# Cross attention scores in 32-row tiles, one query head of each key group at a time, in a two-layer decoder on one core

## The reference

```python
hidden = jnp.concatenate([context, latents], axis=1)
q = (latents @ Wq.T).reshape(b, q_len, H, HD)
k = (hidden @ Wk.T).reshape(b, s_len, KV, HD)
v = (hidden @ Wv.T).reshape(b, s_len, KV, HD)
...
scores = jnp.einsum('bkgqd,bksd->bkgqs', q, k) * scale
attn = jax.nn.softmax(scores.astype(jnp.float32), axis=-1).astype(q.dtype)
out = jnp.einsum('bkgqs,bksd->bkgqd', attn, v)
...
return out @ Wo.T
```

## Time and profile before

| What | Value |
|---|---|
| median of 3 runs | 852.35 us (851.16 to 854.41) |
| the profiled execution, its own time | 849.07 us |
| its span, first to last instruction | 847.3 us |
| instructions | 22622 |
| mean granted TensorE clock | 0.998 of full speed |
| data moved by DMA | 36.77 MB, mean 43 GB/s |
| cross attention trips, from the timeline | about 495 to 830 us |

### The profile page before, as it was taken

One profiled execution on the slowest core, in us unless ns is written; L12 is line 12 of the kernel. 1 busy time (PEld: TensorE's weight loads), 2 busy tenths in 40 slices (PEclk: granted clock), 3 DMA queues, 4 the chain that ended last, 5 costly groups with the idle time before them and its releaser, 6 DMA issues.

```text
span 847.3 us, 22622 instructions
## 1 busy us (share of the span) xinstructions
PE 812.5 (96%) x9288; PEld 673.8 (80%) x9288; DVE 574.4 (68%) x1510; ACT 432.6 (51%) x1109; POOL 262.2 (31%) x310
## 2 busy tenths in 40 slices
PE   6999999999999999999998999999999999999996
PEld 6888887675557787777776789988989899989993
DVE  5675666586876666677776547983767566756776
ACT  4454444568763343465555446634644475347532
POOL 0221522579976532112222567710000100010001
PEclk9999999999999999999999999999999999999999
DMA  8410002222221200010000122320000010000001
GB/s 306 142 53 16 16 22 83 66 70 56 72 63 38 63 22 9 20 29 18 19 19 19 32 62 89 100 65 26 1 2 2 1 50 2 2 1 27 2 2 50
DMA packets 20998, 36.77 MB, mean 43 GB/s; under 512 B 3200, under 2 KB 7424, under 8 KB 20640
## 3 DMA queue, kind: packets, MB, share of 16 engines
q1 hardware_dynamic: 20800, 35.20, 13.6%
q10 hardware_dynamic: 96, 0.13, 0.1%
HBM read 30.86 MB, written 2.10 MB: 39 GB/s over the span
## 4 chain that ended last, share of the span: by engine, by line
PE 78%; DVE 10%; ACT 4%; issue 2%; POOL 2%; DMA 2%; SPq 1%; ACTq 0%; POOLq 0%; DVEq 0%
PE bank L833 18%; PE bank L835 16%; PE bank L834 16%; PE bank L984 6%; PE bank L1259 5%; PE bank L1004 2%; PE bank L1121 2%; DVE tank L2565 2%; PE bank L989 2%; DVE tank L2345 1%; PE bank L954 1%; PE bank L1108 1%; PE bank L1243 1%; DMA x_all<-x_dram 1%; PE bank L1278 1%
## 5 line engine op out<-in xcount | busy, mean ns | idle before, releaser
L833 PE MATMUL bank<-wr,hTl 128*128 128x512 f32 (+3 forms) x392 | 153.5, 391 | 1.3 <-issue 0.8
L835 PE MATMUL bank<-wr,hTh 128*128 128x512 f32 (+3 forms) x392 | 147.0, 375 | 0.0
L834 PE MATMUL bank<-wr,hTh 128*128 128x512 f32 (+3 forms) x392 | 146.6, 374 | 0.0
L1562 ACT ACTIVATE pT<-bank 128x512 f32<-128x512 f32 x128 | 70.0, 605 | 94.9 <-PE bank L954 94.9
L2345 DVE TENSOR_REDUCE tank<-bank 128x4 f32<-128x512 f32 x128 | 82.0, 682 | 42.4 <-PE bank L954 42.4
L833 PEld LDWEIGHTS bank<-wr,hTl 128*128 128x128 f32 (+1 forms) x392 | 73.7, 188 | 17.7 <-issue 5.3
L835 PEld LDWEIGHTS bank<-wr,hTh 128*128 128x128 f32 (+1 forms) x392 | 73.7, 188 | 12.6
L834 PEld LDWEIGHTS bank<-wr,hTh 128*128 128x128 f32 (+1 forms) x392 | 73.8, 188 | 11.3 <-issue 1.0
L833 PE MATMUL bank<-hTh,wr 128*128 128x256 f32 (+1 forms) x272 | 82.0, 302 | 0.0
L834 PE MATMUL bank<-hTl,wr 128*128 128x256 f32 (+1 forms) x272 | 81.3, 299 | 0.0
L835 PE MATMUL bank<-hTh,wr 128*128 128x256 f32 (+1 forms) x272 | 81.2, 298 | 0.0
(11 more groups left out here) (257 smaller groups left out, 1923.8 us busy)
## 6 DMA issues: line engine op xcount, KB each, us to landing
raw<-w_qkv_dram SPq DMA_DIRECT2D x12, 256.0 KB, 2.8
raw<-w_xq_dram SPq DMA_DIRECT2D x16, 192.0 KB, 2.3
raw<-w_xo_dram SPq DMA_DIRECT2D x12, 256.0 KB, 2.8
cin<-xT_dram SPq DMA_DIRECT2D x8, 256.0 KB, 3.6
x_all<-x_dram SPq DMA_DIRECT2D x8, 256.0 KB, 7.0
cin<-ctx_dram SPq DMA_DIRECT2D x8, 256.0 KB, 3.4
cin<-ctxT_dram SPq DMA_DIRECT2D x8, 256.0 KB, 2.9
out_dram<-x_all SPq DMA_DIRECT2D x8, 256.0 KB, 2.0
```

Source lines behind the costliest of these rows:

```text
L833: mm(dst, lhs[1], rhs[0], start=start, stop=False)
L834: mm(dst, lhs[0], rhs[1], start=False, stop=False)
L835: return mm(dst, lhs[0], rhs[0], start=False, stop=stop)
L1562: av(pT[e][:, 2 * rows + n, :], t_bank[n][:, :], ACT.Exp).then_inc(exp_ready, 1)
```

## The change

A turn now takes one query head of each of the four key groups instead of the four heads of one group. The 96 features of a head are cut into three parts of 32, and the weights are put in such an order that a projected tile of 128 rows holds one part of all four groups. The scores of group n then use rows 32n to 32n+31 of the array and have a PSUM bank of their own, `scores_bank(n)`, for both slots: 72 matmuls of 32x256 for each turn. Keys are split once for each trip, with the factor 96^-0.5 already in them, so the maxima are negated in the reduction. The rescaled copy of the maxima, the splits of keys in each turn and the pieces of the fourth head go.

The values of a turn go to `bank[s][2]` (in the last turn `bank[s][0]`), which brings new waits. The kept values of slot 0, n = 1, move behind the queries of turn 1 in trips 1 to 3. The first half of the transposes is copied by VectorE behind its split of the queries, the second by ScalarE; in turn 2 ScalarE's `xT_copied` comes behind these copies, as in the code. In trip 0 the division of slot 1 is shared with ScalarE in every turn, before in turn 0 only. Ahead of `first_pair`, TensorE multiplies a tile of zeros (bf16, 128x512) 17 times.

```diff
...
-WIDE, NARROW = 64, 32
+PART = P // XKV
+PARTS_OF_HEAD = XD // PART
...
+        xk_last = sb("xk_last", [P, 2, SLOTS, XT], F32R)
...
+        xk_parts = [nc.alloc_sbuf_tensor_at(f"xk{c}", [P, 2, SLOTS, XT], F32R, offset=at_tank + 4 * c * TANK) for c in range(2)] + [xk_last]
...
+        xq_parts = [wr[:, at:at + PARTS_OF_HEAD * XT].rearrange("p (c s t) -> p c s t", c=PARTS_OF_HEAD, s=SLOTS) for at in (AT_AL, AT_BL)]
...
+        def rows_of_group(n):
+            return slice(n * PART, (n + 1) * PART)
+        def scores_bank(n):
+            return bank[n // SLOTS][n % SLOTS]
+        def values_bank(s, g):
+            return bank[s][2 if g + 1 < XG else 0]
...
+        CLOCKED = 17
...
+            def keep_clocked():
+                pe.wait_ge(idle_ready, 1)
+                for _ in range(CLOCKED):
+                    mm(t_bank[0][:, :], idle[:, :], idle[:, :].unsqueeze(1).broadcast_to([P, KT, P]), start=True, stop=True, skip_group_check=True)
...
+                        if g > 1:
+                            for s in both:
+                                pe.wait_ge(xo_ready[s], nth(trip, XG, g - 1))
...
+            def cross_scores(trip, g):
+                pe.wait_ge(xk_ready, nth(trip, PARTS_OF_HEAD, PARTS_OF_HEAD))
+                pe.wait_ge(xq_ready, nth(trip, XG, g + 1))
+                for q_lo, k_lo in ((1, 0), (0, 1), (0, 0)):
+                    q = xq_of(trip, g)[q_lo]
+                    for c in range(PARTS_OF_HEAD):
+                        for s in both:
+                            for n in range(XKV):
+                                at = rows_of_group(n)
+                                ins = mm(scores_bank(n)[:, s * XT:(s + 1) * XT], q[at, c, s, :], xk_parts[c][at, k_lo, s, :],
+                                         start=q_lo == 1 and c == 0 and s == 0, stop=q_lo + k_lo == 0 and c + 1 == PARTS_OF_HEAD,
+                                         skip_group_check=True)
+                ins.then_inc(xs_psum, 1)
+            def cross_probsT(trip, s, g):
+                pe.wait_ge(xp_ready[1], nth(trip, 2 * XG, 2 * g + 1 + s))
                 for i in range(2):
+                    pe.wait_ge(xpn_ready[s], nth(trip, 2 * XG, 2 * g + i + 1))
+                    if (trip, s, i) == (0, 1, 1):
+                        pe.wait_ge(first_normed, g + 1)
                     for j in range(4):
                         at = (4 * i + j) * P
                         ins = nc.tensor.transpose(bank[s][i][:, j * P:(j + 1) * P], xp[s][:, at:at + P], ident[:, :])
                     ins.then_inc(xpT_psum[s], 1)
             def cross_values(trip, s, g):
+                pe.wait_ge(xpT_ready[s], nth(trip, 2 * XG, 2 * g + 2))
                 if g == 0:
                     pe.wait_ge(xv_ready[s], nth(trip, 2, 2))
+                if g + 1 < XG:
+                    pe.wait_ge(xq_ready, nth(trip, XG, g + 2))
+                if g + 2 == XG and trip > 0:
+                    pe.wait_ge(xT_hi[s], turned(trip - 1, FF))
+                for c in range(PARTS_OF_HEAD):
                     for t in range(2):
+                        for n in range(XKV):
+                            at = t * NKV + n * XD + c * PART
+                            ins = mm(values_bank(s, g)[rows_of_group(n), c * P:(c + 1) * P], xv[s][:, at:at + PART],
+                                     xpT[s][:, (2 * n + t) * P:(2 * n + t + 1) * P], start=t == 0, stop=t == 1)
                 ins.then_inc(xo_psum[s], 1)
...
             def routes_and_low(trip, s):
                 pe.wait_ge(xT_hi[s], turned(trip, FF))
+                if trip + 1 < TRIPS:
+                    pe.wait_ge(xo_ready[s], nth(trip + 1, XG, XG - 1))
...
+            keep_clocked()
             first_pair()
...
                 cross_keys(trip)
-                if behind:
-                    cross_kept_values(trip, 1, 1)
-                cross_kept_values(trip, 0, 1)
+                cross_kept_values(trip, 1 if behind else 0, 1)
                 for g in range(XKV):
-                    each(cross_scores, trip, g)
+                    cross_scores(trip, g)
                     if g + 1 < XKV:
                         cross_q(trip, g + 1)
+                        if g == 0 and behind:
+                            cross_kept_values(trip, 0, 1)
                     elif behind:
                         each(routes_and_low, trip - 1)
                     if g > 0:
...
             def cross_keys(trip):
                 for n_done, i in enumerate(KEY_TILES):
+                    act.wait_ge(xk_psum, nth(trip, PARTS_OF_HEAD, n_done + 1))
+                    av(xk_parts[i][:, 0, :, :], bank[i % 2][i // 2][:, :].rearrange("p (s t) -> p s t", s=SLOTS), ACT.Copy, scale=XD ** -0.5
+                       ).then_inc(xk_hi, 1)
...
                 hi = xq_of(trip, g)[0]
                 act.wait_ge(xq_psum, n + 1)
                 act.wait_ge(xq_ready, nth(trip, XKV, g))
+                copy(hi[:, 0:2, :, :], two_parts(trip, g))
                 act.wait_ge(xq_psum, n + 2)
+                copy(hi[:, 2, :, :], third_part(trip, g)).then_inc(xq_hi, 1)
+            def cross_probs(trip, g):
+                if (trip, g) == (0, 0):
+                    act.wait_ge(xs_psum, 1)
+                for n, s in ((0, 0), (0, 1), (1, 0), (1, 1), (2, 0), (3, 0), (2, 1), (3, 1)):
+                    act.wait_ge(xmax_ready, nth(trip, XKV * XG, XKV * g + n + 1))
+                    ins = av(xp[s][:, n * XT:(n + 1) * XT], scores_bank(n)[:, s * XT:(s + 1) * XT], ACT.Exp,
+                             bias=st[s][:, NEGMAX.start + n:NEGMAX.start + n + 1], scale=1.0,
+                             accum_out=st[s][:, ROWSUM.start + n:ROWSUM.start + n + 1])
+                    if n % 2 == 1:
+                        ins.then_inc(xp_ready[s], 1)
+            def first_norm(g):
+                act.wait_ge(first_sums, g + 1)
                 for j in range(2, 4):
                     block = xp[1][:, j * XT:(j + 1) * XT]
                     ins = av(block, block, ACT.Copy, scale=st[1][:, ROWSUM.start + j:ROWSUM.start + j + 1])
                 ins.then_inc(first_normed, 1)
+            def second_probsT(trip, s, g):
+                act.wait_ge(xpT_psum[s], nth(trip, 2 * XG, 2 * g + 2))
+                copy(xpT[s][:, 512:1024], bank[s][1][:, :]).then_inc(xpT_ready[s], 1)
             def cross_heads(trip, s, g):
                 act.wait_ge(xo_psum[s], nth(trip, XKV, g + 1))
                 n = XG * XD // P
+                copy(hTh[:, 0:n, s, 0, :], tiles(values_bank(s, g)[:, 0:XG * XD], n)).then_inc(xo_hi[s], 1)
...
                 cross_keys(trip)
-                if behind:
-                    cross_kept_values(trip, 1, 1)
-                cross_kept_values(trip, 0, 1)
+                cross_kept_values(trip, 1 if behind else 0, 1)
                 if trip > 1:
                     each(ff_norm, trip - 2)
                 for g in range(XKV):
-                    each(cross_probs, trip, g)
-                    if g == 0:
-                        cross_split(trip, 0, 1)
+                    cross_probs(trip, g)
+                    if trip == 0:
+                        first_norm(g)
                     if g + 1 < XKV:
                         cross_q(trip, g + 1)
                     elif behind:
                         each(route_exp, trip - 1)
-                    if (trip, g) == (0, 0):
-                        first_norm()
+                    if g == 0 and behind:
+                        cross_kept_values(trip, 0, 1)
+                    each(second_probsT, trip, g)
                     for s in both:
-                        if copied_by_act(trip, s, g):
-                            probsT_by_act(trip, s, g)
-                    for s in both:
-                        if g + 1 < XKV and (g, s) != (0, 0):
-                            cross_split(trip, s, g + 1)
                         if g + 2 == XKV and behind and s == 0:
                             each(xT_copied, trip - 1, 2)
                         cross_heads(trip, s, g)
...
+            nc.gpsimd.memset(idle[:, :], 0.0).then_inc(idle_ready, 1)
...
+                v.tensor_tensor(lo[:, 0:2, :, :], two_parts(trip, g), f32(hi[:, 0:2, :, :]), ALU.subtract)
+                v.tensor_tensor(lo[:, 2, :, :], third_part(trip, g), f32(hi[:, 2, :, :]), ALU.subtract).then_inc(xq_ready, 1)
+            def cross_keys(trip):
+                for n_done, i in enumerate(KEY_TILES):
+                    dve.wait_ge(xk_hi, nth(trip, PARTS_OF_HEAD, n_done + 1))
+                    v.scalar_tensor_tensor(out=xk_parts[i][:, 1, :, :], in0=bank[i % 2][i // 2][:, :].rearrange("p (s t) -> p s t", s=SLOTS),
+                                           scalar=XD ** -0.5, in1=f32(xk_parts[i][:, 0, :, :]), op0=ALU.mult, op1=ALU.subtract
+                                           ).then_inc(xk_ready, 1)
+            def cross_max(trip, g):
+                dve.wait_ge(xs_psum, nth(trip, XG, g + 1))
+                for n in range(XKV):
```

(44 more changed lines are left out.)

112 lines of the change are left out of this document (19 added, 93 removed).

## The result

| | Before | After | Ratio (95%) |
|---|---|---|---|
| first comparison, medians (4 runs each) | 851.75 us | 843.43 us | 0.9904 (0.9886 to 0.9922) |
| both run again, medians (23 and 5 runs) | 852.02 us | 844.31 us | 0.9905 (0.9884 to 0.9927) |
| first profiled executions, own time | 849.07 us | 842.99 us | |
| profiled executions of the repeats, own time | 852.05 us | 845.23 us | |

The change makes the kernel 8 us faster, about 0.95%. The forecast was 4.6 us, 847.8. The result lies in the range, near its lower end.

The account below looks back on a forecast made before the run. TensorE, busy 812.5 of 847.3 us, was taken as the bound. Terms -8.3 - 1.1 + 3.2 + 1.6 = -4.6 us took the profiled 849.07 to 844.5; adding 3.3 to the median gave 847.8, range 842.5 to 853.5.

Parts of the forecast that it names:

- scores, 16 turns: Cross attention scores on four row tiles: stage 2.35 us instead of 2.91, in turn 0 2.45 instead of 2.84; 8.3 us gained.
- transposes, 9 turns: Turns 0, 1 and 3 of trips 1 to 3: ScalarE copying half removes a 0.12 us wait each; 1.1 us gained.
- turn 2, trips 1 to 3: Values of slot 0 wait for ScalarE's `xT_copied`, queued behind `second_probsT`: 3.05 us after the first transpose, not 1.98; 3.2 us lost.
- trip 0, waits: VectorE's slow scalings beside GpSimd delay turns 0 and 3, turn 2's wait goes; 1.6 us lost, bounds 1.3 gained, 4 lost.
- zeros: Before the first pair: zeros may save 1.5 us of slow matmuls, but TensorE then idles waiting for VectorE; nothing gained.
- profiled execution to median, before and after alike: Whole kernel: the median 852.35 lies 3.3 us above the profiled execution, so 844.5 becomes a forecast of 847.8.
- rival C: Scores: rounds are longer because stationary tile loads lie in the open; +9.6, in all +5.0 us, 857.4; chance 0.12.
- one slow pair and the key splits: Turn 2 of trip 0: VectorE's load falls by these, so the 1.28 us wait goes.
- Rival D: Start of the kernel: zeros do bring time, 1.5 us reaching the first scores; -6.1 us, 846.3; chance 0.05.
- A: Cross attention: no new waits of weight, turn 2 waits little and trip 0 nothing; about -9.7 us, 842.7; chance 0.15.
- B: Softmax chain comes late in turns 0 and 3 of every trip, 0.6 us each; about 852; chance 0.20.

Follow-up runs that it names:

- the last run: Kernel after, with VectorE doing all four pairs of scalings in turns 1 to 3 of trip 0 and each maximum negated by its own operation: 850.22 us, ratio 0.9975.

## Why the prediction was wrong

| Term | Forecast | Measured |
|---|---|---|
| scores, 16 turns | -8.3 | -7.3 |
| transposes, 9 turns | -1.1 | -1.3 |
| values | 0 | -0.5 |
| turn 2, trips 1 to 3 | +3.2 | +3.5 |
| trip 0, waits | +1.6 | +0.4 against the first trace, -1.6 against the repeat |
| zeros | 0 | 0 to -1.0 |
| profiled execution to median, before and after alike | +3.3 | +2.7 before, +0.4 after |

- **The scores.** Right in mechanism, with a round at 0.115, so rival C is out. The stage is 2.31, but I counted 0.1 for each of the two changes of tiling inside it, and the second shows up in the queries: (2.91 + 4.10) - (2.31 + 4.20) = 0.50 a turn instead of 0.56. In turn 0 the first change shows in the kept values (2.18 for 12 matmuls, 2.08 elsewhere), and the gain is 0.32, not 0.39. 12 x 0.50 + 4 x 0.32 = 7.3. The Trainium skill's figure of 3.07 for four row tiles with N=512 (TensorE: Matmul & The Clock Gate, "Measured speedup vs the span model"), from which the prediction worked out 0.149 us a round in favour of rival C, does not describe these rounds of N=256: 0.115 for four against 0.114 for one full-array matmul is close to four times.
- **Transposes and values.** 1.98 to 1.84, nine times, is 1.3. The values went from 2.80 to 2.76 in the twelve turns where the next stage is now on row tiles and no longer on 96 rows; in turn 3, where the full array follows, they took 2.76 in both kernels. I had no term for it.
- **The wait in turn 2.** Right in place and cause: 3.16 for a forecast of 3.05. Moving the two copies of x ahead brought 4.0 us by the stages (3 x 1.32) and 4.6 between the medians.
- **Trip 0 failed.** The sum had 1.6 us lost there; it was 0.4 lost against the first trace and 1.6 gained against the repeat. "The transposes stage becomes 5.3 instead of 2.89": it is 4.20, VectorE's three pairs took 0.86, 0.94 and 0.62 there (517.23 to 520.19), not 1.5 each. And the execution of before that I read was itself a lucky one. Against the repeat the stages of trip 0 differ by 4.20 - 3.62 in turn 0, -0.5 in the scores of turn 2 (3.42 in the repeat, 2.92 in the first trace), where those of slot 1 wait for VectorE's part of the heads, 1.84 - 3.95 in turn 2 and 2.37 - 1.98 in turn 3, together -1.6. I gave the credit for turn 2 to "one slow pair and the key splits". The pair was hidden. With it and the four tiny negations of a turn back, trip 0 loses 6.9 us, 2.3 of them by the clock, while with the pair alone it loses nothing. The wait in turn 2 is back as well then, at 2.77 instead of 1.84 us for the stage. The list of what the change takes away had the rescaled copies of the maxima, but I gave them no price of their own. The splits of keys in each turn were not put back by any run, so their share in the waits of before is not shown.
- **The step to the median failed.** "The median of the runs, 852.35, lies 3.3 above that execution, so I forecast 847.8" carried a difference over as if it were a property of measuring. It was the waits of trip 0 that the good execution did not have (2.24 us in the trace of the repeat), and these the change takes away. After's median lies 0.4 above its profiled execution; in the repeats the median lies 0.0 from it in before and 0.9 below it in after, so the distance is no constant of either kernel. Which of the tiny operations meets GpSimd differs from run to run, but why the first execution waited less in all is open: its 18 operations of 128x2 took 5.3 us in trip 0 and its 30 scalings 18.9, against 5.5 and 18.3 in the repeat. The step from execution to median is 2.9 of the 4.4 us between 847.8 and 843.4. Of the other 1.5 (844.5 to 842.99) trip 0 is 1.2 and the start 0.4, the terms of the stages together give 0.6 the other way, and some 0.5 I can't place.
- **Zeros.** "The 1.5 us become idle time" held only for the execution that I read. Rival D's mechanism was right, at up to 1.0 us in the traces. For D's 1.5 the evidence is the comparison in before alone (0.2%, 1.5 us); in after it is 0.6, within the spread.
- **Rivals A and B.** A's time (842.7) is about what came out, but by luck and not for its reason: the waits of turn 2 are all there. B did not occur. With the kept values ahead of the scores again it does, in turn 0.

## What to carry to other kernels

A tiny scaling on VectorE in SBUF can cost what is left of the GpSimd instruction that it meets, here up to 1.30 us for 0.17. So count such operations one by one wherever GpSimd runs long ones, and fold them into the instruction before them (here the negation into the reduction, the scale into the keys). The kernels without them also had the steadier times here. And count what a wait of TensorE may cost behind it: here the stage behind it lost 0.7 to 1.7 us to the clock in some cases and nothing in others. Before carrying a distance between a profiled execution and the median over to the changed kernel, ask which stretch varies and whether the change removes it; two traces of the same kernel show it. When a bank gets a new user, look at what its reader stands behind in its queue: here one swapped line was worth half as much as the whole change.

## What the runs showed of the hardware that I had not expected

- VectorE's scalings from SBUF to SBUF waited for the GpSimd instruction that they met. In trip 0 of the last run the stretched ones of 128x2 end within 0.03 us of it, the stretched ones of 128x256 within 0.15 of it; those of 128x2 averaged 0.49 us, with a longest of 1.30, against 0.17. A subtraction with both inputs in SBUF was stretched too (0.41 to 0.82 us, L2552 in the trace of before at 525.10). Maxima read from PSUM stayed at 0.68, and reciprocals, which also go from SBUF to SBUF, at 0.15 to 0.17.
- TensorE's granted clock fell while the engine was busy without a gap: 72 matmuls of 32 rows that go round the four row tiles run at 1.00, the same 72 one tile at a time at 0.78, with 0.50 in their last 3 us, and the stage behind them at 0.57.
- It also fell to 0.62 behind a wait of 2.13 us, and the values there took 4.42 us instead of 2.76; behind the 1.53 us in after (522.92) they still took 2.76, and behind 1.80 in the repeat of before (558.07) 2.80. In the last run waits of 0.90, 0.26 and 1.02 us in one turn (521.00 to 523.57) were followed by 0.79 in the values. So the length of the last wait alone did not decide it.
- A change between the full array and row tiles cost 0.1 us on either side, and both show in the stages of the full array: the last matmul ahead of the scores is followed after 0.27 us (591.48 to 591.75) instead of 0.17, and the queries behind them take 0.1 us more.
